# A fused attention and mixture-of-experts layer on one core: exponentials placed between key copies, two chunks of mixed keys interleaved, gates moved into a layer norm

## The reference, cut to what matters

```python
x = x + xattn(layernorm(x), ctx)   # 16 heads of 64, 257 context rows of width 384 per batch
x = x + attn(layernorm(x))         # 16 heads of 32, one shared projection for q, k and v
x = x + ffn(layernorm(x))          # 8 experts, top 2: gates, gelu(x w1 + b1) w2 + b2, layer norm
```

## Time and profile before

| what | value |
|---|---|
| median of 3 runs | 1377.63 us (1376.15 to 1378.84) |
| profiled execution | 1379.4 us, its span 1377.8 us |
| mean granted TensorE clock | 0.979 |
| TensorE busy | 1275.2 us, 93% of the span |
| VectorE busy | 1033.0 us, 75% |
| ScalarE busy | 886.8 us, 64% |
| GpSimd busy | 218.8 us, 16% |
| the attention groups | from about 11 to 757 us of the span |
| one turn of the group loop | 91.5 us |

### The profile page before, as it was taken

The page is one execution under the profiler, slowest core; times in us unless marked ns, Lnnn a source line. Parts: engine busy times, 40 slices in busy tenths (PEclk is TensorE's granted clock), DMA queues, the critical chain, the costliest instruction groups (busy, mean ns, idle before and its releaser), DMA issues.

```text
span 1377.8 us, 26640 instructions
## 1 busy us (share of the span) xinstructions
PE 1275.2 (93%) x8320; PEld 839.6 (61%) x8321; DVE 1033.0 (75%) x2246; ACT 886.8 (64%) x1434; POOL 218.8 (16%) x265
## 2 busy tenths in 40 slices
PE   5898999999999999999999789999999999999990
PEld 5767668677696686876966544555555555555540
DVE  5675777877877778768676668878787878787875
ACT  3577776676777776767777245666666666666650
POOL 1001002021020020210200221212121212121102
PEclk9999999999999999999999899999999999999995
DMA  9436246164372451642715991862626265511104
GB/s 364 151 115 237 95 144 224 65 223 156 110 252 86 155 211 65 236 158 98 252 62 187 361 358 36 311 247 78 247 79 245 80 243 196 192 23 23 23 9 129
DMA packets 71107, 224.77 MB, mean 163 GB/s; under 512 B 5718, under 2 KB 5956, under 8 KB 64916
## 3 DMA queue, kind: packets, MB, share of 16 engines
q1 hardware_dynamic: 64704, 210.03, 41.9%
q0 software_dynamic: 6336, 14.24, 5.0%
q10 hardware_dynamic: 28, 0.01, 0.0%
HBM read 177.78 MB, written 46.48 MB: 163 GB/s over the span
## 4 chain that ended last, share of the span: by engine, by line
PE 60%; issue 18%; DVE 9%; DMA 6%; ACT 3%; POOL 2%; SPq 0%; ACTq 0%; DVEq 0%; POOLq 0%
PE bank L748 6%; PE bank L749 6%; PE bank L750 6%; PE bank L728 6%; PE bank L729 6%; PE bank L730 6%; PE bank L1648 5%; PE bank L738 3%; DMA w_halves<-moe_w 2%; PE bank L1632 2%; DMA w_halves<-arena 2%; PE bank L1694 2%; PE bank L1683 2%; PE bank L1686 2%; PE bank L1707 2%
## 5 line engine op out<-in xcount | busy, mean ns | idle before, releaser
L1648 PE MATMUL bank<-moe_w 128*128 128x257 f32 x768 | 189.6, 384 | 0.0
L1648 PEld LDWEIGHTS bank<-moe_w 128*128 128x128 f32 x768 | 137.6, 191 | 18.7 <-ACT moe_w L1059 0.9
L728 PE MATMUL bank<-moe_w,arena 128*128 (+1 forms) x368 | 139.5, 379 | 0.7 <-DVE arena L591 0.7
L729 PE MATMUL bank<-moe_w,arena 128*128 (+1 forms) x368 | 139.5, 379 | 0.0
L730 PE MATMUL bank<-moe_w,arena 128*128 (+1 forms) x368 | 139.5, 379 | 0.0
L476 ACT ACTIVATE wosT<-moe_w,now_v_act 128x1024 f16 (+1 forms) x92 | 100.7, 1141 | 27.2 <-PE bank L750 27.2
L1066 ACT ACTIVATE moe_w<-bank,cols,ugain 128x512 f32<-128x512 f32 x96 | 74.6, 777 | 62.6 <-PE bank L1695 61.8
L546 DVE SCALAR_TENSOR_TENSOR arena<-bank,now_b,arena 128x512 f32<-128x512 f32 x92 | 68.9, 749 | 52.4 <-PE bank L730 48.2
L1291 DVE TENSOR_TENSOR moe_w<-bank,moe_w 128x512 f16<-128x512 f32 (+1 forms) x96 | 65.4, 688 | 48.7 <-ACT moe_w L1080 46.4
L421 POOL DMA_INDIRECT acc_rows<-arena,job_idx x23 | 36.7, 1597 | 393.8 <-DVE arena L623 393.8
L469 ACT ACTIVATE arena<-bank,now_h 128x512 f16<-128x512 f32 x92 | 63.5, 691 | 50.8 <-PE bank L738 35.2
(11 more groups left out here) (272 smaller groups left out, 3118.7 us busy)
## 6 DMA issues: line engine op xcount, KB each, us to landing
moe_w<-in_L_ffn_w_dram SPq DMA_DIRECT2D x46, 1024.0 KB, 6.3
moe_w<-w_halves SPq DMA_DIRECT2D x8, 4096.0 KB
moe_w<-in_L_ffn_w_dram SPq DMA_DIRECT2D x8, 4096.0 KB
w_halves<-moe_w SPq DMA_DIRECT2D x48, 512.0 KB, 3.9
arena<-in_ctx_dram SPq DMA_DIRECT2D x32, 384.0 KB
arena<-in_L_ffn_w_dram SPq DMA_DIRECT2D x10, 1024.0 KB, 5.1
blocks<-in_L_ffn_w_dram SPq DMA_DIRECT2D x8, 1024.0 KB, 4.8
arena<-in_L_ffn_b_dram SPq DMA_DIRECT2D x8, 1024.0 KB
```

The costliest lines, as they stand in the source:

```text
L728: nc.tensor.matmul(bank[fb % 2][:, :], xT_low[:, k, :], high, start=(k == 0), stop=False)
L729: nc.tensor.matmul(bank[fb % 2][:, :], xT_high[:, k, :], high, start=False, stop=False)
L1648: last = nc.tensor.matmul(bank[h][:, 0:KEYS], qkT[:, c, b, h * P:(h + 1) * P], cnT[:, b % 2, c, :], start=(c == 0), stop=(c == KC - 1))
```

## The change

Three edits, all in the order of the work:

1. In the first batch of a group, `exps` of head group k stands right behind key copy k on ScalarE for k = 0, 1, 2, and only the last head group behind them. The wait for `halves_out[3]` moves from behind the three key copies to behind the first. VectorE norms the heads in three pieces: 0 and 1 after `row_max` 2, head 2 after `row_max` 3, head 3 behind that, with a reciprocal for each piece.
2. In the fifth pass TensorE does the four high matmuls of chunk 0, the four of chunk 1, the `ct_fill` for chunk 1, then the three low ones of chunk 0 and of chunk 1. Chunk 2 is as before. ScalarE's order is not changed.
3. `gates` moves from behind `ln_apply` to between `ln_stats` and `ln_apply`; the first two operations of `place` (now `place_first`) go ahead of `ln_stats`; `first_id` moves to second place within `gates`.

```diff
@@ ScalarE
-            def exps(g, b):
+            def exps(g, b, heads=range(HG)):
                 bt = GB * g + b
-                for h in range(HG):
+                for h in heads:
...
                             n_hi(g, 0, k)
                             ct_out(tp(g, ("ct", 1, k)), 1, k)
+                            if do_b and k == 0:
+                                act.wait_ge(halves_out[3], 32 * g)
+                            exps(g, 0, [k])
...
-                    if do_a and do_b and b == 0:
-                        act.wait_ge(halves_out[3], 32 * g)
                     if do_a and b < GB:
-                        exps(g, b)
+                        exps(g, b, [HG - 1] if b == 0 else range(HG))
@@ VectorE
             def norm_probs(g, b):
                 bt = GB * g + b
-                dve.wait_ge(exp_done, HG * (bt + 1))
-                nc.vector.reciprocal(rinv[:, :], rsum[:, :]).then_inc(rinv_done, 1)
-                dve.wait_ge(rinv_done, bt + 1)
-                for h in range(HG):
+                norm_heads(bt, 0, HG, (GB + 2) * g + b + 2).then_inc(norm_done, 1)
+
+            def norm_heads(bt, first, end, before):
+
+                dve.wait_ge(exp_done, HG * bt + end)
+                nc.vector.reciprocal(rinv[:, first:end], rsum[:, first:end]).then_inc(rinv_done, 1)
+                dve.wait_ge(rinv_done, before + 1)
+                for h in range(first, end):
...
                             row_max(g, b, k)
+                            if b == 0 and k >= 2:
+                                norm_heads(GB * g, 0 if k == 2 else 2, k, (GB + 2) * g + k - 2)
...
-                        if b in (0, 3):
+                        if b == 0:
+                            norm_heads(GB * g, HG - 1, HG, (GB + 2) * g + 2).then_inc(norm_done, 1)
+                            n_lo(g, b)
+                        elif b == GB - 1:
                             norm_probs(g, b)
                             n_lo(g, b)
...
-                    layernorm(ln, x_all[:, bass.ds(g, 1), :].rearrange("p g d -> p (g d)"), y[:, :], y_done)
+                    x_now = x_all[:, bass.ds(g, 1), :].rearrange("p g d -> p (g d)")
+                    if do_b:
+                        place_first(g - 1)
+                    ln_stats(ln, x_now)
+                    if do_b:
+                        gates(g - 1)
+                    ln_apply(ln, x_now, y[:, :], y_done)
+                elif do_b:
+                    gates(g - 1)
+                    place_first(g - 1)
                 if do_b:
-                    gates(g - 1)
                     place(g - 1)
@@ TensorE
-                        if do_a and (1 <= b < 3 or (b == GB and nxt and c > 0)):
+                        if do_a and b == GB and c == 0:
+                            av_high(g, b - 1, 0)
+                            av_high(g, b - 1, 1)
+                            if nxt:
+                                ct_fill(tp(g, ("ct", GB, 1)), GB * g + GB, GB, 1)
+                            av_low(g, b - 1, 0)
+                            av_low(g, b - 1, 1)
+                        if do_a and (1 <= b < 3 or (b == GB and nxt and c > 1)):
```

More of the change, by code:

```diff
@@ L1278, in norm_probs @@
                 bt = GB * g + b
-                dve.wait_ge(exp_done, HG * (bt + 1))
-                nc.vector.reciprocal(rinv[:, :], rsum[:, :]).then_inc(rinv_done, 1)
-                dve.wait_ge(rinv_done, bt + 1)
-                for h in range(HG):
+                norm_heads(bt, 0, HG, (GB + 2) * g + b + 2).then_inc(norm_done, 1)
[4 more added lines that the diff above has]
+                for h in range(first, end):
                     last = nc.vector.tensor_scalar(probs[:, h, :], probs[:, h, :], rinv[:, h:h + 1], P_SCALE, ALU.mult, ALU.mult)
-                last.then_inc(norm_done, 1)
+                return last
             def pt_lo(g, b, k):
@@ L1526, in gates @@
                 link(nc.vector.tensor_scalar(gsum[:, :], ge[:, :], 1.0, None, ALU.add))
+                nc.vector.scalar_tensor_tensor(out=first_id[:, :], in0=ids[:, bass.ds(g, 1)], scalar=float(-TOKENS), in1=mask[:, 0:1],
+                                               op0=ALU.add, op1=ALU.mult)
                 link(nc.vector.reciprocal(entry_f[:, 0, 1:2], gsum[:, :]))
@@ L1529, in gates, with place_first @@
                 nc.vector.tensor_copy(entry[:, :, 0], ids[:, bass.ds(g, 1)].to_broadcast([P, TOPK]))
-                nc.vector.scalar_tensor_tensor(out=first_id[:, :], in0=ids[:, bass.ds(g, 1)], scalar=float(-TOKENS), in1=mask[:, 0:1],
-                                               op0=ALU.add, op1=ALU.mult)
-            def place(g):
+            def place_first(g):
                 dve.wait_ge(b_full, B_FILLS * g + RK_AT + 1)
@@ L1537, in place @@
                 nc.vector.tensor_tensor(next_row[:, :], BK[:, EXPERTS:2 * EXPERTS], next_row[:, :], ALU.add).then_inc(b_free, 1)
+            def place(g):
                 dve.wait_ge(b_free, 1 + B_FILLS * (g + 1))
@@ L1673, in pt_fill, with av_high @@
                 last.then_inc(full, 1)
[L1675 to L1679, removed]
+            def av_high(g, b, c):
+                n, columns = GB * g + b, slice(c * P, (c + 1) * P)
+                ps = m_open(g, ut_at(b, c))
                 for k in range(2):
@@ L1686, in av, with av_low @@
                     nc.tensor.matmul(ps[:, :], n_low[:, b, k, columns], pT_high[:, k, :], start=False, stop=False)
+            def av_low(g, b, c):
+                ps, columns = M[ut_at(b, c) % 2], slice(c * P, (c + 1) * P)
                 if c == 0:
@@ L1696, in av @@
                                  start=False, stop=True).then_inc(m_full, 1)
+            def av(g, b, c):
+                av_high(g, b, c)
+                av_low(g, b, c)
             def o_proj(g, i):
@@ L1827, in body @@
                     for c in range(KC):
-                        if do_a and (1 <= b < 3 or (b == GB and nxt and c > 0)):
+                        if do_a and b == GB and c == 0:
[6 more added lines that the diff above has]
+                        if do_a and (1 <= b < 3 or (b == GB and nxt and c > 1)):
                             nb = b + 1 if b < GB else GB
                             ct_fill(tp(g, ("ct", nb, c)), GB * g + nb, nb, c)
-                        if do_a and b >= 1:
+                        if do_a and (1 <= b < GB or (b == GB and c > 1)):
                             av(g, b - 1, c)
```

## The result

The changed kernel takes 1366.68 us in the median of 4 runs (1365.64 to 1368.46), the kernel before 1377.74 (1376.15 to 1378.84) beside it: a ratio of 0.9917, 95% interval 0.9904 to 0.9931. That is 11.1 us less; 10.6 were forecast. A second set of the same kernel gave 1366.88, ratio 0.992 (0.9904 to 0.9937). The profiled execution took 1366.68, its span is 1365.1.

The account below looks back on a forecast made before the run. TensorE, busy 91.7 of 95 us, bounds the kernel, so only its idle time can be won. Group 0's 0.5, groups 1 to 6's 7.9 and group 7's 2.2 make 10.6: 1377.63 to 1367.0 us, range 1364.5 to 1370.

Parts of the forecast that it names:

- Part 1, 0.58: First batch, exponentials between key copies and norm in three pieces: 0.58 us saved a turn, between nothing and 0.75.
- the new stall: First batch: the late second key copy on ScalarE makes TensorE wait 0.22 us at the `ct_fill`.
- the one product left: End of the first batch's norm: one product of about 0.34 us behind the last reciprocal instead of 1.14, 0.80 less.
- Part 2, 0.04: Fifth pass, two chunks interleaved: TensorE 0.66 us earlier there, but only 0.04 saved in a turn.
- later next to nothing: Behind the fifth pass: TensorE gains 0.19 us at `wo_proj`, then almost none, since VectorE sets the turn's end.
- Part 3, 0.74: Turn's end on VectorE, gates in the layer norm's hole: 0.74 us less up to the `qT` copy, between 0.63 and 0.90.
- The edges: First and last groups: 0.5 us saved in group 0, 2.2 in group 7, which has no next group.
- Part 2 through: Rival: the fifth pass's gain survives every turn, 0.6 us more in each of 7, 1362.7 us; chance 0.10.
- Part 1 eaten: Rival: TensorE loses at `ct_fill` what it won at `pt_fill`, 7 x 0.58 comes back, 1371.1 us; chance 0.14.
- Stores last: Rival: late `halves_out[3]` stores hold up ScalarE's exponential 0, 1388 us if landing at 324.0; chance, with similar waits, 0.05.
- Table loads: Rival: loads around the three exponentials among key copies on ScalarE, 7.7 us a group, 1428 us; chance 0.01.
- The tail's clock: Rival: less idle keeps TensorE's key projection after the last turn at the higher clock, 2 us more, 1365; chance 0.06.

Follow-up runs that it names:

- part 3 alone: Only the gates moved into the layer norm's hole, with two additions ahead of the statistics, on the kernel before: 1373.51 us beside 1377.52, ratio 0.9971.
- `b1` run: Kernel before with ScalarE's one-time row sum of `b1` moved ahead of the last weight split in group 0: 1376.25 us beside 1377.28, ratio 0.999.
- part 2 or 3 alone: Two kernels, each with one edit on the kernel before: chunks 0 and 1 interleaved in the fifth pass, 1376.68 us; gates in the layer norm's hole, 1373.51 us.

## Why the prediction was right

The time (1367.0 against 1366.68) and the turn (90.2 against 90.13 to 90.18) came out as forecast, and so did each part's mechanism. Two terms were mis-sized, in opposite directions, and the total hides differences of the clock in groups 0 and 1 that weren't foreseen.

- **What bounds.** TensorE's idle time is what could be won: over one turn it fell from 3.29 (91.50 less 88.21 busy) to 1.50 (90.14 less 88.64), and the turn by 1.37. The 0.43 between them is busy time, whose ends the profile models. The waits of the earlier trace rows were the right list.
- **Part 1, 0.58: measured 0.41 alone.** Where it acts it gave 0.53: from the third `qk_proj` to the first `pt_fill` it was 16.73 us (309.87 to 326.60) and is 16.20 (304.65 to 320.85). ScalarE's idle (0.96 for 1), the new stall (TensorE takes 0.23 longer from its scores to `ct_fill`, for 0.22) and the one product left (0.35 for 0.34) were sized right, and no wait for the stores appeared. The other 0.12 is lost late in the turn: VectorE's copy of the row sums (`L1312` changed) and the gate's logits behind it (`L1471`) start 0.22 apart where before and with part 3 alone it is 0.11, with no releaser in the row. It is 0.22 in the steady turns of all nine profiles that have part 1, and 0.11 in the four without. Its cause is open.
- **Part 2, 0.04: measured 0.16 to 0.18.** The 0.3 left in the fifth pass (0.23), the new wait of 0.4 ahead of `wo_proj` (0.32) and ScalarE's longer idle (0.52 to 1.25) were right. The step that was mis-sized is "later next to nothing", with its reason, "VectorE in turn works without a break that TensorE could shorten". VectorE has such a break, the `yT` copy that waits 1.43 us for TensorE (0.81 in the changed kernel), and so has ScalarE, through which the gain came: ScalarE's copy of the layer-normed input waits for TensorE's `xn_fill` and comes 0.15 earlier behind the pass's first `pt_lo` (17.36 to 17.21 us), and the row scales, the weight split and VectorE's end follow (23.33 to 23.18). This reading is from the traces; no run moved that copy by itself.
- **Part 3, 0.74: measured 0.75 on VectorE.** From the last residual addition to the `qT` copy it was 5.70 us (392.06 to 397.76) and is 4.95 (296.10 to 301.05). Both waits at `qk_proj` are gone. The turn gave 0.79 alone.
- **The edges.** Group 7 with the tail gave 1.85 for 2.2: `y_fill` came 2.09 us earlier behind the `qT` copy (87.16 to 85.07), and the key projection behind it took 0.35 longer. Group 0 gave 0.55 for 0.5, but that nearness is luck. Its key projections (64 matmuls) took 4.02 us for 5.47, with a granted clock of 1.00 for 0.72 in 34 to 40 us, and its `wo_proj` 8.83 for 7.14. The `b1` run is the fairer partner, with the changed kernel's times in both places and the order of before up to the output projection: against it the end of the mixed keys comes 0.40 earlier in group 0, 0.49 by part 1 (0.58 forecast) less 0.09 by part 2 (0.1 forecast). The start lost 0.69, which no part touches: over the thirteen profiled executions it lasted 16.61 to 18.07 us. The four with 17.7 or more have the 4.02 behind it, the nine with 17.3 or less the 5.47. What sets it is not known.
- **Group 1.** The sum holds none of its surplus of 2.7 us, and no term for a clock that differs. In the medians the surplus seems smaller, by an estimate that sets single profiled executions against medians: without the surplus the measured stretches make 12.7 - 2.7 = 10.0, against 11.1, which leaves 1.1 for group 1. The profiled execution of before lay 1.7 above its median, which is the rest. So the forecast came out near by right terms, and within half a microsecond by luck: what the start lost and group 1 gave too much nearly cancel.
- **The rivals.** Part 2 through: no, until the row scales were moved, and then 0.69 a turn by the mechanism given. Part 1 eaten: the stall was 0.23, not 0.58. Stores last: no store releases an exponential (the store that releases ScalarE at the turn's end was there before, for 2.94 us, and is now 2.44). Table loads: none appeared among copies and exponentials, so what the Trainium skill says of identity and copy being in every set ("ScalarE: Activation LUTs", section "Table sets: the hidden batching unit") agrees with this trace. The tail's clock: the key projection behind the last turn still runs slowly, 6.65 us where it took 6.30, with a granted clock of 0.55 in 748 to 755 us, although the idle ahead of the fill fell from 2.1 to 1.52. The timeline of the changed kernel there, and the window:

```profile
746.31 0.63 PE L1762 MATMUL bank<-ident,y 128*128 128x128 f32 x4 [1.52 <-DVE y L1227]
748.40 6.65 PE L1769 MATMUL bank<-yT,moe_w 128*128 128x128 f32 x32 [1.46 <-DVE yT L1271]
```

```profile
748.00:755.00 7.00, 6.60 (x32) 6.46 (x32) 4.86 (x3) 4.35 (x6) 4.96 (x5) 0.55 1.02 407
```

## What to carry to other kernels

Before you fill an idle stretch of the bounding engine, follow the next in-order engine that it meets again: 0.7 us won in the fifth pass was worth 0.18 while a row-scale chain stood ahead of the output projection, and 0.69 once two lines of VectorE's order were swapped. Look for holes that a helper engine leaves (here GpSimd's power): moving other small work into one gave 0.79 us a turn, into another 0.23. Measure edits of some tenths of a microsecond by the length of the steady turn, but don't take the sum of the turns for the gain until the median shows it: groups 0 and 1, with their changing clock, differed by up to 4.8 us between kernels that were 0.18 apart in a turn, and one edit that shortened six turns by 2.8 us left the median of four runs where it was.

## What the runs showed of the hardware

- A stretch at the lower clock under another engine's work can be hidden behind a later wait. The `wo_proj` of group 0 took 8.83 us for 7.14, and with part 2 or 3 alone the third key projection of group 1 still started 107.75 and 107.79 us behind group 0's `qT` copy, for 107.84 before, its wait for ScalarE 0.48 and 0.63 instead of 2.34.
- Nearly the same program fell into either of two patterns: group 1 of 93.4 to 94.6 us, or of 96.0 to 98.5.
- A shorter wait may give more than its own length. Moving the row scales removed 0.32 of wait and 0.51 of the turn; some 0.2 of it lay between `rk_fill` and `q_proj` (0.25 apart, then 0.08), where no wait row names it.
- Two small instructions of VectorE (`L1312`, `L1471`), with no releaser in their rows, were 0.11 apart in the steady turns of the four kernels without part 1 and 0.22 in those with it.
